# Causal mask folded into the spare rows of the maxima product, with a corner of 32 keys left, in an attention and mixture-of-experts block on one core

## The chip, the cores and the metric

The program runs on one core of a Trainium2 chip. The metric is device time in microseconds from start to end. Engines: TensorE (PE) does matrix products and transposes into PSUM, VectorE (DVE) and ScalarE (ACT) work on rows, GpSimd (POOL) does set-up work and indexed transfers, SyncE (SP) issues the other transfers.

## What is computed

One transformer block over 4 sequences of 256 tokens, width 256, 16 heads of 16, followed by 64 experts of which each token uses 8. Cut to what matters here:

```python
scores = jnp.einsum('bhqd,bhkd->bhqk', Q, K) / scale
causal = jnp.tril(jnp.ones((S, S), dtype=bool))
scores = jnp.where(causal, scores, jnp.float32(-jnp.inf))
attn = jax.nn.softmax(scores, axis=-1)
out = jnp.einsum('bhqk,bhkd->bhqd', attn, V)
...
h = _layernorm(x, axis=-1) * (1 + cb) + sb
x = x + gb * _L0_ffn_ref(h, ...)   # router, top 8 of 64 experts, silu(g) * u, down
```

## The kernel before, in words

Each engine has its own program, and semaphores order them. A prologue converts constants, normalises the first batch and projects its queries, keys and values. Batches 0 to 2 then run in rounds: a round finishes the attention of one batch and prepares the next (`one_round`, twice in a loop, then `last_round`). The attention of the last batch (3) is done tile by tile (`last_scores`, `last_values`). When all token rows are scattered by expert, the experts run, and their outputs are summed.

**Maxima.** Scores are first computed with queries on partitions (`scores_for_max`, under the mask `maskb`), and DVE takes the maximum of each row and head. `split_maxima` writes the negated maxima as a high and a low bfloat16 part to `neg2`, 2 x 16 columns of 128; the other 96 columns were set to zero once in the prologue. `neg_transposes` turns them on PE, so that row 16 c + h of the result belongs to part c of head h. ACT copies the result to `negT` in `negs` (in the last batch `last_negs`, a tile at a time).

**Scores for the values.** `attend` computes the scores once more with keys on partitions. For each of four groups of four heads it fills three PSUM banks: two with two heads each for key tile 0 (256 queries a head), one with four heads for key tile 1 (128 queries a head). In each bank PE first adds the mask to the diagonal tiles of all heads in one product (`identb` with `maskTb` broadcast over the heads), then for each head the product of keys and queries and the product of `pickb` with `negT`, which subtracts the maximum: `pickb[:, h, :]` has ones in rows h and 16 + h, in every column, and zeros elsewhere. In `attend` the mask product covers 256 columns in the banks of two heads (128 each) and 512 in the banks of four. ACT takes the exponential of each bank (`softmax`; line 684), and the banks rotate over three. `pv` on PE multiplies with the values. Between the groups ACT also does two steps for the next batch (`high`, lines 673 and 674) and copies results out (line 691).

In the last batch `last_scores` does the same for banks of four heads and one tile, with a mask product of 512 columns in the eight banks on the diagonal (line 1131), and ACT takes the exponential in `last_exp` (line 782).

**Prologue.** GpSimd converts the constants from `cst`: identity, the two masks, a prefix matrix, and `pickb` (2048 elements a row, one instruction, line 537); then it signals `g_csts`, which PE waits for before the first `neg_transposes`. In the same stretch DVE runs `rope_tile` (lines 1402, 1405, 1407) and `low` (1413, 1414) for the two tiles of batch 0. Line 1402 and 1405 read one input from PSUM and one from SBUF; 1407, 1413 and 1414 read both inputs from SBUF. PE then does the transposes of `split_transposes` (line 965), the modulation columns (line 926) and the first scores (981, 984), in that order. `link` makes an engine wait for the instruction that it is given before the next one starts.

## Time and profile before

| what | value |
|---|---|
| time, median of three runs (lowest to highest) | 316.97 us (316.59 to 317.23) |
| profiled execution, its own time | 318.18 us |
| span of that execution | 316.4 us |
| busy share PE / PE weight loads / DVE / ACT / POOL | 89% / 66% / 65% / 50% / 50% |
| mean granted clock of PE | 0.94 of 2.4 GHz |
| shares of the chain that ended last | PE 59%, DVE 15%, issue 9%, DMA 7%, ACT 4% |

A timeline lists instructions in order of time: start, duration, engine, line, operation, output and input, shape, count; in brackets the idle time of the engine before it and what ended it. Several like instructions in a row stand as one row with a count, and its duration runs from the first start to the last end. The duration of a product on PE includes its way through the array, so how long one holds PE is read from the start of the next. The granted clock is given as a share of 2.4 GHz, so 0.50 is 1.2 GHz.

### The profile page before, as it was taken

What the parts mean: (1) busy time and instruction counts of PE and PEld (TensorE: products, weight loads), DVE (VectorE), ACT (ScalarE), POOL (GpSimd) and SP (SyncE); (2) the same over time, 40 slices, a digit from 0 to 9 for tenths busy, and PEclk for the clock granted to TensorE, in tenths of its full rate; (3) what the DMA queues carried; (4) which work ended last, traced back from release to release, by engine and by line L of the source; (5) the groups of instructions that cost most, each with busy time, mean ns of one, the idle gap of its engine ahead of it and who ended that gap; (6) DMA issues with size and microseconds to landing.
All of it is one profiled execution on the core that took longest, in us unless ns stands there. A gap on an engine that the chain in (4) does not pass through costs nothing.

```text
span 316.4 us, 7008 instructions
## 1 busy us (share of the span) xinstructions
PE 282.7 (89%) x2094; PEld 208.7 (66%) x2094; DVE 205.1 (65%) x627; ACT 158.4 (50%) x462; POOL 157.7 (50%) x154
## 2 busy tenths in 40 slices
PE   6989999998999899768772759999999999999994
PEld 3478567566766667527431348888888888777883
DVE  3494876878788958852261125677777778994186
ACT  4454378545863585433621225666666666693000
POOL 1810000002555445646476564778887778888300
PEclk9795999999999999975997697999999999999999
DMA  6790099999999997992196356899998999866883
GB/s 216 260 312 1 14 309 333 338 382 294 265 265 305 312 253 223 312 322 107 58 293 204 90 137 177 169 211 192 158 163 154 181 168 153 106 75 74 178 273 133
DMA packets 63657, 64.61 MB, mean 204 GB/s; under 512 B 5069, under 2 KB 60562, under 8 KB 63632
## 3 DMA queue, kind: packets, MB, share of 16 engines
q1 hardware_dynamic: 52928, 49.07, 54.8%
q0 software_dynamic: 10704, 15.24, 25.9%
q8 instruction: 12, 0.20, 0.3%
q14 instruction: 13, 0.11, 0.1%
HBM read 35.93 MB, written 28.84 MB: 205 GB/s over the span
## 4 chain that ended last, share of the span: by engine, by line
PE 59%; DVE 15%; issue 9%; DMA 7%; ACT 4%; another core or an unknown queue 3%; POOL 1%; SPq 1%; ACTq 0%; DVEq 0%; POOLq 0%
PE bank L1280 11%; PE bank L1294 8%; PE bank L953 5%; PE bank L1271 4%; PE bank L1013 3%; PE bank L984 2%; PE bank L965 2%; PE bank L1059 2%; PE bank L1288 2%; PE bank L1029 2%; PE bank L1027 2%; PE bank L981 2%; PE bank L1024 2%; DMA arena<-in_wmod 2%
## 5 line engine op out<-in xcount | busy, mean ns | idle before, releaser
L603 POOL DMA_INDIRECT slot_rows<-stage x48 | 48.0, 999 | 37.1 <-issue 8.3
L1280 PE MATMUL bank<-arena,stage 128*128 (+1 forms) x256 | 54.1, 334 | 1.3 <-issue 1.3
L637 POOL DMA_INDIRECT sum<-kz,stage x26 | 40.1, 1542 | 10.5 <-issue 5.8
L1280 PEld LDWEIGHTS bank<-arena,stage 128*128 128x128 f32 x256 | 41.0, 194 | 2.5 <-issue 1.8
L1294 PE MATMUL bank<-arena,stage 96*128 (+1 forms) x128 | 41.0, 403 | 0.4 <-issue 0.4
L854 ACT ACTIVATE stage<-bank 128x256 f32<-128x256 f32 x64 | 24.5, 382 | 23.7 <-issue 14.6
L1430 DVE TENSOR_REDUCE rmax<-bank 128x2 f32<-128x512 f32 (+1 forms) x48 | 30.9, 686 | 7.7 <-PE bank L984 7.3
L1651 DVE SCALAR_TENSOR_TENSOR stage<-stage,bank 128x96 f32<-128x96 f32 x64 | 16.2, 253 | 24.5 <-ACT stage L864 14.1
L592 POOL COPY stage<-slot_idx 128x16 uint32<-128x16 uint32 x2 | 0.4, 196 | 59.0 <-DVE slot_idx L1529 59.0
L637 POOL DMA_INDIRECT sum<-stage x17 | 26.3, 1545 | 6.0 <-issue 3.4
L1271 PE MATMUL bank<-cst,stage 128*128 128x128 f32 x128 | 25.3, 278 | 1.3 <-DMA stage<-slot_rows 0.8
L953 PE MATMUL bank<-arena 128*128 128x512 f32 (+1 forms) x64 | 25.1, 516 | 0.5 <-ACT arena L667 0.4
L861 ACT ACTIVATE stage<-bank 128x96 f32<-128x96 f32 x64 | 16.0, 250 | 19.0 <-PE bank L1280 10.3
L1271 PEld LDWEIGHTS bank<-cst,stage 128*128 128x128 f32 x128 | 17.5, 143 | 9.9 <-issue 2.5
L1325 PE MATMUL bank<-arena 128*128 128x256 bf16 x216 | 23.7, 272 | 0.0
L1325 PEld LDWEIGHTS bank<-arena 128*128 128x128 bf16 x216 | 20.9, 97 | 2.8
L1294 PEld LDWEIGHTS bank<-arena,stage 96*128 96x128 f32 x128 | 19.4, 191 | 4.3 <-issue 0.6
L684 ACT ACTIVATE arena<-bank 128x512 f32<-128x512 f32 x36 | 20.0, 598 | 3.2 <-PE bank L1029 2.7
L981 PE MATMUL bank<-stage 128*128 128x256 bf16 (+1 forms) x48 | 16.4, 342 | 3.8 <-DVE rmax L1430 3.8
L984 PE MATMUL bank<-kz,arena 128*128 128x128 f16 (+1 forms) x128 | 19.8, 267 | 0.0
L612 POOL DMA_INDIRECT slot_rows<-rows,slot_idx x16 | 15.6, 972 | 8.5 <-issue 4.6
L1288 PE MATMUL bank<-cst,stage 128*96 128x128 f32 x64 | 18.0, 281 | 1.7 <-issue 1.0
(209 smaller groups left out, 607.6 us busy)
## 6 DMA issues: line engine op xcount, KB each, us to landing
slot_rows<-zero_row SPq DMA_DIRECT2D x8, 1040.0 KB, 12.1
stage<-slot_rows SPq DMA_DIRECT2D x64, 130.0 KB
arena<-in_gate_up SPq DMA_DIRECT2D x10, 768.0 KB
arena<-in_down SPq DMA_DIRECT2D x5, 768.0 KB
sum<-zero_row SPq DMA_DIRECT2D x3, 1152.0 KB, 13.0
arena<-sum SPq DMA_DIRECT2D x12, 256.0 KB, 4.8
arena<-in_gate_up SPq DMA_DIRECT2D x2, 864.0 KB
arena<-in_wmod SPq DMA_DIRECT2D x1, 1024.0 KB, 6.1
```

Source lines behind the costliest of these rows:

```text
L603: pool.indirect_dma_start(slot_rows, bass.IndirectOffsetOnAxis(ap=idx[:, t, k:k + 1], axis=0), src[:, t, :], None, bounds_check=last_slot, ...
L637: pool.indirect_dma_start(sums[a], where, ye_ring[e % RING], None, compute_op=ALU.add).then_inc(added[a], 16)
L854: nc.scalar.activation(xeT[:, j % 2, :], bank[j % 2][:, 0:HC * CAP], ACT.Copy).then_inc(a_xeT, 1)
L953: mm(dst, h1T[:, k, t * P:(t + 1) * P], wqkv_sb[:, k, c0:c1], start=k == 0, stop=False)
L981: mm(view[:, :, w - P:w], identb, maskb[:, None, :].broadcast_to([P, len(heads), P]), start=True, stop=False, skip_group_check=True)
L984: last = mm(view[:, i, :], qT[:, h // 2, qt * P:(qt + 1) * P], kz[:, h, 0:w], start=False, stop=i == len(heads) - 1, skip_group_check=True)
L1271: last = nc.tensor.transpose(dst, xe[:, j, k * P:(k + 1) * P], ident)
L1280: last = mm(bank[2 + q % 2][:, 0:GU + 1], xeT[:, q % 2, k * CAP:(k + 1) * CAP], expert_w[:, s - 1, k * (GU + 1):(k + 1) * (GU + 1)], start ...
L1288: nc.tensor.transpose(bank[4 + q % 2][0:I, 0:CAP], hid[:, q % 2, :], ident).then_inc(p_hidT, 1)
L1294: mm(bank[6 + q % 2][:, 0:H], hidT[:, q % 2, :], expert_w[0:I, s - 3, HC * (GU + 1):EW], start=True, stop=True).then_inc(p_ye, 1)
L1325: last = mm(dst, picked[:, n, of:of + P], y[:, n, :], start=n == 0 and y is own_high, stop=b < B - 1 and n == NPICK - 1 and y is own_low)
L1430: V.tensor_reduce(rmax[:, qt, h0:h0 + 2 * nh - 1:2], src, AX.X, ALU.max).then_inc(v_max, 1)
```

## The change

`pickb` gets ones of the identity in rows 32 to 127, for every head: row k is 1 in column k. `negT` becomes three slots of 128 columns: slot 0 for queries of tile 0, slot 1 for queries of tile 1 against keys of tile 0, slot 2 for queries of tile 1 against keys of tile 1. Rows 0 to 31 hold the maxima as before; rows 32 to 127 hold the transposed mask in slots 0 and 2 and zeros in slot 1. So the product that subtracts the maximum also masks the keys 32 to 127. Keys 0 to 31 hold a masked query only among the first 32 queries of a diagonal tile; for these a product `corner` adds the mask, 32 columns a head, behind the first head's product of keys and queries, which now opens the bank.

`neg2` has 32 columns, its zeroing on DVE is gone, the transposes write 32 rows, and ACT copies 32 rows: slots 0 and 1 in one instruction, slot 2 in another (in the last batch slot 0, and later 1 and 2). PE waits for the second copy before the first bank that reads slot 2. GpSimd fills the mask rows of `negT` and converts `pickb` in three pieces.

```diff
+    NEG = 2 * NH
...
-        neg2 = early([TPB, P // NH, NH], BF16)
-        negT = early([S], BF16)
+        neg2 = early([TPB, 2, NH], BF16)
+        negT = early([TPB + 1, P], BF16)
...
-            nc.gpsimd.tensor_copy(pickb[:, :, :], cst[:, 4 * P:4 * P + NH, None].broadcast_to([P, NH, P])).then_inc(g_csts, 1)
+            nc.gpsimd.tensor_copy(negT[:, 0, :], cst[:, 2 * P:3 * P])
+            link(nc.gpsimd.tensor_copy(negT[:, TPB, :], cst[:, 2 * P:3 * P]))
+            link(nc.gpsimd.tensor_copy(pickb[0:NEG, :, :], cst[0:NEG, 4 * P:4 * P + NH, None].broadcast_to([NEG, NH, P])))
+            link(nc.gpsimd.tensor_copy(pickb[NEG:2 * NEG, :, :], cst[NEG:2 * NEG, None, 0:P].broadcast_to([NEG, NH, P])))
+            link(nc.gpsimd.tensor_copy(pickb[2 * NEG:P, :, :], cst[2 * NEG:P, None, 0:P].broadcast_to([P - 2 * NEG, NH, P])))
+            nc.gpsimd.memset(negT[:, 1, :], 0.0).then_inc(g_csts, 1)
...
-                nc.scalar.activation(negT, bankb[0][:, 0:S], ACT.Copy).then_inc(a_negT, 1)
+                neg = bankb[0][0:NEG, 0:S].rearrange("p (t q) -> p t q", t=TPB)
+                nc.scalar.activation(negT[0:NEG, 0:TPB, :], neg, ACT.Copy).then_inc(a_negT, 1)
+                nc.scalar.activation(negT[0:NEG, TPB, :], neg[:, 1, :], ACT.Copy).then_inc(a_negT, 1)
...
+            def corner(view, n):
+
+                mm(view[:, :, 0:NEG], identb, maskTb[:, None, 0:NEG].broadcast_to([P, n, NEG]),
+                   start=False, stop=False, skip_group_check=True)
+
             def attend(b):
 
-                pe.wait_ge(a_negT, b + 1)
+                pe.wait_ge(a_negT, TPB * b + 1)
...
-                        mm(view[:, :, 0:P], identb, maskTb[:, None, :].broadcast_to([P, len(heads), P]),
-                           start=True, stop=False, skip_group_check=True)
+                        if (g, kt) == (0, 1):
+                            pe.wait_ge(a_negT, TPB * b + 2)
+                        neg = negT[:, 0:TPB, :].rearrange("p t q -> p (t q)") if kt == 0 else negT[:, TPB, :]
                         for i, h in enumerate(heads):
                             mm(view[:, i, :], kz[:, h, kt * P:(kt + 1) * P], qT[:, h // 2, kt * P:S],
-                               start=False, stop=False, skip_group_check=True)
-                            last = mm(view[:, i, :], pickb[:, h, :], negT[:, kt * P:S],
+                               start=i == 0, stop=False, skip_group_check=True)
+                            if i == 0:
+                                corner(view, len(heads))
+                            last = mm(view[:, i, :], pickb[:, h, :], neg,
...
-                if t == kt:
-                    mm(view, identb, maskTb[:, None, :].broadcast_to([P, 4, P]),
-                       start=True, stop=False, skip_group_check=True)
...
+                    if t == kt and i == 0:
+                        corner(view, 4)
...
-            pe.wait_ge(a_negT, B + 1)
+            pe.wait_ge(a_negT, TPB * (B - 1) + 3)
...
-            link(V.memset(neg2[:, :, :, :], 0.0))
```

GpSimd in the prologue, before; `stage` and `arena` are the buffers that hold the converted constants:

```order
L532 MEMSET arena 128x32 [waits v_zeroed]
L533 CAST stage<-cst 128x128
L534 CAST stage<-cst 128x128
L535 CAST stage<-cst 128x128
L536 CAST stage<-cst 128x128
L537 CAST stage<-cst 128x2048
L542 COPY arena<-router_sb 128x32 [waits wo_and_router_loaded]
```

and after:

```order
L537 CAST stage<-cst 128x128
L538 CAST stage<-cst 128x128
L539 CAST stage<-cst 128x128
L540 CAST stage<-cst 32x2048 [waits gpsimd_chain]
L541 CAST stage<-cst 32x2048 [waits gpsimd_chain]
L542 CAST stage<-cst 64x2048 [waits gpsimd_chain]
L543 MEMSET stage 128x128 [waits gpsimd_chain]
L548 COPY arena<-router_sb 128x32 [waits wo_and_router_loaded]
```

In the place of one conversion of 2048 elements a row stand two of 128 elements, three of 2048 and a memset, and the long ones wait for one another (`gpsimd_chain`).

PE in the first bank of `attend` and the start of the second, before; `stage` holds `identb`, `pickb`, `negT`, the mask, `arena` the queries, `kz` the keys:

```order
L1024 MATMUL bank<-stage 128x2x128 [waits neg_max_T_ready]
L1027 MATMUL bank<-arena,kz 128x256
L1029 MATMUL bank<-stage 128x256
L1027 MATMUL bank<-arena,kz 128x256
L1029 MATMUL bank<-stage 128x256
L1024 MATMUL bank<-stage 128x2x128
```

and after:

```order
L1042 MATMUL bank<-arena,kz 128x256 [waits neg_max_T_ready]
L1008 MATMUL bank<-stage 128x2x32
L1046 MATMUL bank<-stage 128x256
L1042 MATMUL bank<-arena,kz 128x256
L1046 MATMUL bank<-stage 128x256
L1042 MATMUL bank<-arena,kz 128x256
L1008 MATMUL bank<-stage 128x2x32
```

The mask product of 256 columns at the head of the bank has become one of 64 columns in second place; the number of products in a bank is the same.

## Rows read from the trace of the kernel before

**Rows 1.** Timeline of PE in the second attend: start us, us, engine, line, operation.
```profile
73.98 0.28 PE L1024 MATMUL bank<-stage 128*128 128x256 bf16 x1 [0.48 <-ACT stage L744]
74.10 0.27 PE L1027 MATMUL bank<-arena,kz 128*128 128x256 f16 x1
...
75.08 0.38 PE L1024 MATMUL bank<-stage 128*128 128x512 bf16 x1
75.30 0.22 PE L1027 MATMUL bank<-arena,kz 128*128 128x128 f16 x1
75.35 0.22 PE L1029 MATMUL bank<-stage 128*128 128x128 bf16 x1
```

**Rows 2.** Timeline of ACT in the second attend.
```profile
73.54 0.38 ACT L744 ACTIVATE stage<-bank 128x256 bf16<-128x256 bf16 x1 [2.58 <-PE bank L993]
74.74 3.56 ACT L684 ACTIVATE arena<-bank 128x512 f32<-128x512 f32 x6 [0.81 <-PE bank L1029]
...
79.24 1.71 ACT L684 ACTIVATE arena<-bank 128x512 f32<-128x512 f32 x3
...
82.36 1.57 ACT L684 ACTIVATE arena<-bank 128x512 f32<-128x512 f32 x3
```

**Rows 3.** All instructions of line 684: count, then shortest/median/longest in ns.
```profile
L684 ACT ACTIVATE arena<-bank x36: 585/597/618, 42.5 to 116.1; 128x512 f32<-128x512 f32 x36
```

**Rows 4.** Timeline of PE just before the second attend, products of 64 columns.
```profile
71.16 0.19 PE L1093 MATMUL bank<-stage,onesb 128*128 128x64 bf16 x1
71.19 0.19 PE L1092 MATMUL bank<-stage 128*128 128x64 bf16 x1
```

**Rows 5.** Timeline of PE in the last batch.
```profile
145.25 0.63 PE L1131 MATMUL bank<-stage 128*128 128x512 bf16 x1
145.68 0.31 PE L1134 MATMUL bank<-arena,kz 128*128 128x128 f16 x1
```

**Rows 6.** The chain that ended last, in the last batch: start us, us, what.
```profile
153.40 0.59 ACT arena L782
```

**Rows 7.** Timeline of POOL in the prologue.
```profile
6.88 0.28 POOL L507 CAST arena<-arena 8x128 bf16<-8x128 f32 x1 [5.88 <-DMA arena<-in_bias]
...
14.43 0.29 POOL L536 CAST stage<-cst 128x128 bf16<-128x128 f32 x1
14.66 1.89 POOL L537 CAST stage<-cst 128x2048 bf16<-128x2048 f32 x1
```

**Rows 8.** Timeline of DVE in the prologue.
```profile
14.66 0.88 DVE L1405 TENSOR_TENSOR arena<-bank,rope_sb 128x256 f32<-128x256 f32 x2
15.58 1.52 DVE L1407 TENSOR_TENSOR arena<-arena 128x512 f32<-128x512 f32 x1
...
19.50 0.69 DVE L1413 TENSOR_TENSOR arena<-arena 128x512 f16<-128x512 f32 x1
...
21.55 0.69 DVE L1414 TENSOR_TENSOR arena<-arena 128x512 f16<-128x512 f32 x1
...
34.11 0.17 DVE L1570 TENSOR_SCALAR rs<-mv 128x4 f32<-128x4 f32 x1 [0.62 <-ACT arena L753]
```

**Rows 9.** All instructions of line 1407, shortest/median/longest in ns.
```profile
L1407 DVE TENSOR_TENSOR arena<-arena x8: 692/693/1516, 15.6 to 111.4; 128x512 f32<-128x512 f32 x8
```

**Rows 10.** Timeline of PE in the prologue.
```profile
22.30 1.54 PE L965 MATMUL bank<-stage,arena 128*128 128x128 f16 x16 [0.18 <-DVE arena L1414]
23.63 3.52 PE L926 MATMUL bank<-condT,arena 128*128 128x4 f32 x16
```

**Rows 11.** Timeline of ACT in the prologue.
```profile
30.63 1.02 ACT L667 ACTIVATE arena<-bank,modT 128x256 f32<-128x256 f32 x2 [4.33 <-PE bank L943]
```

**Rows 12.** PE by stretch: us, PE busy (instructions), granted clock, DMA share, GB/s.
```profile
22.50:23.00 0.50, 0.50 (x11) 0.72 0.81 243
...
32.50:33.00 0.50, 0.50 (x3) 0.54 0.00 0
...
149.00:149.50 0.50, 0.50 (x11) 0.98 0.17 58
```

More of the change, by code:

```diff
@@ L792, in last_negs @@
                 act.wait_ge(p_negT, B + t)
-                q = slice(t * P, (t + 1) * P)
-                nc.scalar.activation(negT[:, q], bankb[(3, 0)[t]][:, q], ACT.Copy).then_inc(a_negT, 1)
+                neg = bankb[(3, 0)[t]][0:NEG, t * P:(t + 1) * P]
+                for slot in ((0,), (1, TPB))[t]:
+                    nc.scalar.activation(negT[0:NEG, slot, :], neg, ACT.Copy).then_inc(a_negT, 1)
             def one_round(it, more):
@@ L992, in neg_transposes @@
                 for t in range(TPB):
-                    last = nc.tensor.transpose(bankb[0][:, t * P:(t + 1) * P],
+                    last = nc.tensor.transpose(bankb[0][0:NEG, t * P:(t + 1) * P],
                                                neg2[:, t, :, :].rearrange("p c h -> p (c h)"), identb)
                 last.then_inc(p_negT, 1)
+            def corner(view, n):
+                mm(view[:, :, 0:NEG], identb, maskTb[:, None, 0:NEG].broadcast_to([P, n, NEG]),
+                   start=False, stop=False, skip_group_check=True)
             def attend(b):
-                pe.wait_ge(a_negT, b + 1)
+                pe.wait_ge(a_negT, TPB * b + 1)
                 n = 0
@@ L1129, in last_scores @@
                 view = bank[1 + n % 2 if n < 4 else 4 + n % 3][:, :].rearrange("p (h q) -> p h q", q=P)
-                if t == kt:
-                    mm(view, identb, maskTb[:, None, :].broadcast_to([P, 4, P]),
-                       start=True, stop=False, skip_group_check=True)
                 for i, h in enumerate(groups[g]):
                     mm(view[:, i, :], kz[:, h, kt * P:(kt + 1) * P], qT[:, h // 2, t * P:(t + 1) * P],
-                       start=t != kt and i == 0, stop=False, skip_group_check=True)
-                    last = mm(view[:, i, :], pickb[:, h, :], negT[:, t * P:(t + 1) * P],
+                       start=i == 0, stop=False, skip_group_check=True)
+                    if t == kt and i == 0:
+                        corner(view, 4)
+                    last = mm(view[:, i, :], pickb[:, h, :], negT[:, t + kt, :],
                               start=False, stop=i == 3, skip_group_check=True)
@@ L1159, in last_neg_transposes @@
                     pe.wait_ge(a_rows, B - 1)
-                nc.tensor.transpose(bankb[(3, 0)[t]][:, t * P:(t + 1) * P],
+                nc.tensor.transpose(bankb[(3, 0)[t]][0:NEG, t * P:(t + 1) * P],
                                     neg2[:, t, :, :].rearrange("p c h -> p (c h)"), identb).then_inc(p_negT, 1)
@@ L1180, in last_round @@
                 scores_for_max(it, 8, 9, b)
-                pe.wait_ge(a_negT, B)
+                pe.wait_ge(a_negT, TPB * (B - 1) + 1)
                 last_scores(0)
```

## The prediction

> **What bounds the kernel now.** I read the chain that ended last first, then the timelines of TensorE (PE), ScalarE (ACT), VectorE (DVE) and GpSimd (POOL) in the three places that the change touches, and last the granted clock. The attention part (about 10 to 165 us) is one chain of dependent steps that passes from engine to engine; the expert part starts when the last rows are scattered. So a microsecond gained or lost on that chain should reach the end, and one gained beside it should not.
>
> In one call of attend PE begins at 73.98, right behind ACT's copy of the negated maxima [rows 1, 2]. A product of 256 columns holds PE 0.11 us, one of 128 columns 0.055, and the mask product of 512 columns 0.22 (75.08 to 75.30) [rows 1]. One group of four heads, which is three banks, takes PE two times 5 x 0.11 plus 0.22 plus 8 x 0.055, so 1.75 us. ACT takes the exponentials of the same banks, 0.59 each [rows 3], with some overlap. The last three of the call took 1.57 in all [rows 2], so they came every (1.57 - 0.59) / 2 = 0.49: ACT's own pace. The first six took 3.56, one every (3.56 - 0.59) / 5 = 0.59, which is PE's pace, 1.75 / 3. The middle three took 1.71, one every 0.56. So attend is bound by PE in its first half and by ACT in its second, and the two are close.
>
> In the prologue the chain runs over DVE. It rotates and splits queries and keys (14.66 to 22.24) [rows 8]; PE then transposes them, does the modulation columns and the first scores without a gap (from 22.30 on) [rows 10].
>
> **The change in attend.** Every bank loses a mask product over all its columns and gets a corner of 32 columns a head. A bank of two heads goes from 256 to 64 columns, one of four heads from 512 to 128. A product of 64 columns, with a weight load of its own, is followed by the next one 0.03 us later [rows 4], one of 128 columns 0.055 later [rows 1]. The number of weight loads is unchanged. So PE saves 0.08 on each of eight banks and 0.16 on each of four, 1.28 us for one attend. A group then costs PE 1.43, which is just under ACT's 3 x 0.49 = 1.47: ACT is late next, and what comes out is what ACT lost to PE. That is 0.08 at the first bank, 6 x (0.575 - 0.49) = 0.51 over the first six (3.45 from first start to the end at ACT's pace, 3.56 less one overlap of 0.1), and about 0.13 over the middle three. Together 0.72, **2.2 us less** for three calls. The bounds are 3 x 0.08 = 0.25 (ACT's spacing is its own) and 3 x 1.28 = 3.8 (all of PE's saving counts); I stay with the value between, since the last three show ACT's pace with its banks ready.
>
> The price there is a second copy on ACT, for the third slot of negT. The copy of 256 columns takes 0.38 and ends at 73.92; the first exponential starts at 74.74 [rows 2]. The new one has half the columns, costs 0 to 0.38 and lies inside these 0.82 us. Only the third bank waits for it, and PE is there about 0.9 us after the first copy. Queued behind it on ACT is the first exponential, which waits for PE anyway. I count nothing; in the last batch, where PE waits for both copies before the fifth bank, it may cost up to 0.38 and has PE's transposes beside it. The transposes that now write 32 rows stream as many columns as before: nothing. The removed memset on DVE is worth 0 to 0.17 (the shortest DVE operation in [rows 8]); I count nothing.
>
> **The change in the last batch.** Eight mask products of 512 columns become corners of 128. The one at 145.25 stands in a stretch at half clock and holds PE 0.43 [rows 5]; a quarter of that is 0.11, so it saves 0.32. Two more stand ahead of the exponential at 153.40, for which the chain waits [rows 6], at 0.22 - 0.055 = 0.16 each. Together **0.65 us less**. The other five stand beside waits for other engines; in full they would give 5 x 0.16 = 0.8 more, which I keep as a bound.
>
> **The change in the prologue.** GpSimd used to convert pickb in one instruction of 1.89 us [rows 7]. Now it is three, for 32, 32 and 64 rows, each with the same 2048 elements a row, each waiting for the one before. The time goes by elements in a row and not by rows: 8 rows of 128 took 0.28, 128 rows of 128 took 0.29 [rows 7]. So I take 1.89 for each. Ahead of them come two more conversions of 128 columns, 0.24 apart. GpSimd thus works from 14.66 to about 21.5 and not to 16.55.
>
> That costs because of one row of DVE. The addition in line 1407 has both inputs in SBUF; it takes 0.69 normally [rows 9], and took 1.52 at 15.58, while GpSimd's conversion ran until 16.55 [rows 7, 8]. It ended at 17.10, 0.55 after that conversion: it was held until GpSimd was through. The operations of line 1405, which read one input from PSUM, ran at 14.66 beside the same conversion at 0.44 each [rows 8], and were not held.
>
> Worked out for the new order: the first conversion runs from 15.26 to 17.15, and the addition, ready at 15.58, ends at 17.7 and not 17.1. The second conversion waits for it and runs to about 19.45. The next addition, ready at 19.36, gets through by 20.05; the third conversion starts then and ends at 21.85. The subtractions of lines 1413 and 1414, both inputs in SBUF, were to start at 20.1: the first is held and ends at 22.4. The last ends at 24.4, where it ended at 22.24: 2.2 us. If GpSimd never waits for DVE, the second addition is held instead, and the same 2.2 comes out. The bounds are 0 and 2.8 (held at every one of the three conversions).
>
> The Trainium skill, SBUF — State Buffer, section Who interferes with whom, has a rule that speaks against this change: a VectorE instruction with two SBUF inputs and a GpSimd instruction that reads SBUF exclude each other, and whichever starts first keeps the port for its whole length. The trace agrees with 1.52 against 0.69 in one direction; no row here shows the other. By the rule the delay is the 2.2 above; were the port shared by halves, each held operation would lose half its overlap, and it would be about 1.
>
> Then PE. Its clock falls to 1.2 GHz at 22.7, after PE had waited for DVE, and is back at 2.4 GHz at 32.95 [rows 12]. Both groups of 16 transposes now lie wholly in the slow stretch, at 0.107 each (0.43 / 4, [rows 5]), so the modulation columns start at 23.1 + 3.4 = 26.5 and not 23.63 [rows 10], 2.9 late. If the clock comes back at 32.95 as before, the first scores and the transposes behind them catch up a little: ACT's step at 30.63 [rows 11] begins about 33.15, DVE's step at 34.11 [rows 8] as much later, and attend begins **2.4 us later**. If the clock comes back later by as much as the work is late, it is 3.1.
>
> **The clock in the last batch.** There PE is at 1.2 GHz until 149.0 [rows 12]. The work is 2.4 - 2.2 = 0.2 late there; a rise that stays at 149.0, as I took the one at 32.95 to stay, leaves 0.2 us less of dense work at half speed, **0.1 less**.
>
> **The sum.** +2.4 - 2.2 - 0.65 - 0.1 = -0.55, some -0.5. The profiled execution took 318.18 with a span of 316.4, so it would be 317.7; against the median of the three runs, 316.97, it is **316.5 us**, no change, or just faster. A measurement of this kernel can tell about 0.2%, 0.63 us, from no change.
>
> **The rivals.** (1) In attend the saving lies beside ACT: its spacing of 0.59 is its own, and only the first bank counts. +2.4 - 0.25 - 0.65 = +1.5, so 318.5, slower. For it: ACT is hardly ever idle there; against it: 0.49 in the last three. It decides from the point where the first six exponentials still take over 3.4. (2) The clock's rise follows the work in the prologue: +3.1 - 2.2 - 0.65 = +0.25, 317.2, the same. For it: both rises came in dense work; against it: nothing in the rows ties them to the program. (3) GpSimd's conversions hold DVE hardly at all, and the one long addition was chance. Then -2.2 - 0.65 = -2.85, of which a rise at 149.0 that stays takes back up to half of 2.2: 314.1 to 315.2, faster. Against it is that the addition ended just behind GpSimd. (4) The five other masks of the last batch count too: -0.55 - 0.8 = -1.35, 315.6, faster. Against it: PE pauses in those stretches. That the change does not bring what it says is rival 1.
>
> **Chances.** The forecast 0.34 (its own range is 315.9 to 317.1); rival 1 0.18; rival 2 0.17; rival 3 0.14; rival 4 0.17. Faster: 0.13 of the forecast, 0.14 of rival 3, 0.15 of rival 4, that is 0.42. Slower: 0.16 of rival 1, 0.06 of rival 2, that is 0.22. The rest, 0.36, is the same. The range, 315.0 to 318.3, takes in rivals 2 and 4 whole, the near ends of rivals 1 and 3, and the bounds next to them.
>
> **What would show it.** In the trace after: three long conversions on GpSimd and, beside them, additions and subtractions of DVE that take over 1 us; the last subtraction ending near 24.4; the first attend starting 2.4 later; the first six exponentials in about 3.0; some 9.2 us from attend's first product to its last exponential's end and not 9.95 (73.98 to 83.93). The forecast is wrong if DVE ends near 22.3, if attend keeps its length, or if the clock's edges move with the work.

## The result and the profile after

The first comparison gave 324.22 us as the median of four executions of the changed kernel (322.40 to 325.78), against 317.1 for the kernel before (four executions, 316.59 to 321.58); the ratio is 1.0203, with an interval of 1.0142 to 1.0263. The profiled execution of the changed kernel took 322.4 us with a span of 320.5, where the one of before had 318.18 and 316.4. Four later comparisons, with both kernels timed in turn on one chip each, give much less: ratios of 0.9974, 0.9968, 1.0072 and 1.0041, on average 1.0014, and differences of means from -0.04% to +0.9%, with a weighted mean of **+1.2 us and a standard error of 0.4**. (The ratios leave out executions more than 1.5% above a kernel's fastest; the differences of means take in all but one stray one.) The four sets differ by more than their own errors (-0.1 ± 0.7 and +3.0 ± 0.8 us at the ends), so the 0.4 is too narrow. The change thus brings no gain: it makes the kernel slower by 0.1 to 0.4%, which isn't clear of nothing by the ratios, and the larger part of the first figure belongs to that set of executions.

The page of after, first its head, then TensorE's and GpSimd's busy time (share of the span, instructions):

```profile
span 320.5 us, 7016 instructions
...
PE 279.2 (87%) x2094; PEld 207.4 (65%) x2094; DVE 205.6 (64%) x626; ACT 157.6 (49%) x466; POOL 163.0 (51%) x159
```

TensorE is busy 3.5 us less than before and GpSimd 5.3 more: both halves of the change are there. Where the two stand in the prologue, GpSimd first, then DVE (start us, us, engine, line, operation), after:

```profile
15.53 1.89 POOL L540 CAST stage<-cst 32x2048 bf16<-32x2048 f32 x1
17.48 2.23 POOL L541 CAST stage<-cst 32x2048 bf16<-32x2048 f32 x1
19.77 2.31 POOL L542 CAST stage<-cst 64x2048 bf16<-64x2048 f32 x1
...
15.77 2.19 DVE L1423 TENSOR_TENSOR arena<-arena 128x512 f32<-128x512 f32 x1
...
19.64 0.69 DVE L1423 TENSOR_TENSOR arena<-arena 128x512 f32<-128x512 f32 x1
20.36 2.27 DVE L1429 TENSOR_TENSOR arena<-arena 128x512 f16<-128x512 f32 x1
...
24.02 0.69 DVE L1430 TENSOR_TENSOR arena<-arena 128x512 f16<-128x512 f32 x1
```

These answer to [rows 7, 8]. The additions and subtractions of 0.69 take 2.19 and 2.27 where a conversion is running, and the conversions of 1.89 take 2.23 and 2.31 where DVE is ahead. The last subtraction ends at 24.71 (before: 22.24). TensorE behind it, after:

```profile
18.69 1.95 PE L935 MATMUL bank<-condT,arena 128*128 128x4 f32 x16
23.53 3.57 PE L974 MATMUL bank<-stage,arena 128*128 128x128 f16 x32 [2.89 <-DVE arena L1430]
26.90 3.52 PE L935 MATMUL bank<-condT,arena 128*128 128x4 f32 x16
30.28 0.59 PE L990 MATMUL bank<-stage 128*128 128x512 bf16 x1
```

It now waits 2.89 us for DVE, all 32 transposes run at half clock, and the modulation columns begin at 26.90, where they began at 23.63 [rows 10]. The granted clock is the last number but two, after:

```profile
32.50:33.00 0.50, 0.50 (x6) 0.50 (x5) 0.38 (x1) 0.00 (x0) 0.00 (x0) 0.50 0.00 0
36.00:36.50 0.50, 0.50 (x2) 0.17 (x2) 0.43 (x3) 0.47 (x2) 0.00 (x0) 0.76 0.00 0
```

So TensorE is back at 2.4 GHz at 36.2, not at 32.95 as before [rows 12]. ScalarE in the second attend, after:

```profile
76.20 0.37 ACT L751 ACTIVATE stage<-bank 32x256 bf16<-32x256 bf16 x1 [2.58 <-PE bank L1002]
76.48 0.25 ACT L752 ACTIVATE stage<-bank 32x128 bf16<-32x128 bf16 x1
77.30 3.04 ACT L690 ACTIVATE arena<-bank 128x512 f32<-128x512 f32 x6 [0.57 <-PE bank L1046]
...
81.32 1.55 ACT L690 ACTIVATE arena<-bank 128x512 f32<-128x512 f32 x3
...
84.24 0.60 ACT L697 ACTIVATE arena<-bank 128x512 f32<-128x512 f32 x1 [0.33 <-PE bank L1027]
84.74 1.57 ACT L690 ACTIVATE arena<-bank 128x512 f32<-128x512 f32 x3
```

Against [rows 2] the six exponentials take 3.04 and not 3.56, the next three 1.55 and not 1.71; but ahead of the last three there is now a pause of 0.33.

How the lateness of the profiled execution develops (after less before): +2.47 at the last subtraction, +3.26 at the first copy of negated maxima on ACT, +2.46 at the third, +1.81 at ACT's first step behind the third attend, +2.35 at the last exponential of the last batch, +2.64 where the last slots (the places of the token rows among the experts) are ready, +2.95 at ACT's first copy for the experts, +4.1 at the end. ACT at these points, the first copy, the third, the step behind the third attend and the last exponential, before:

```profile
40.69 0.38 ACT L744 ACTIVATE stage<-bank 128x256 bf16<-128x256 bf16 x1 [4.24 <-PE bank L993]
...
106.00 0.38 ACT L744 ACTIVATE stage<-bank 128x256 bf16<-128x256 bf16 x1 [2.58 <-PE bank L993]
...
126.72 0.20 ACT L656 ACTIVATE rs<-rs 128x2 f32<-128x2 f32 x1 [3.06 <-DVE rs L1479]
...
155.63 0.58 ACT L782 ACTIVATE arena<-bank 128x512 f32<-128x512 f32 x1
```

and after:

```profile
43.95 0.37 ACT L751 ACTIVATE stage<-bank 32x256 bf16<-32x256 bf16 x1 [4.24 <-PE bank L1002]
...
108.46 0.37 ACT L751 ACTIVATE stage<-bank 32x256 bf16<-32x256 bf16 x1 [2.63 <-PE bank L1002]
...
128.53 0.20 ACT L662 ACTIVATE rs<-rs 128x2 f32<-128x2 f32 x1 [3.05 <-DVE rs L1495]
...
157.98 0.58 ACT L790 ACTIVATE arena<-bank 128x512 f32<-128x512 f32 x1
```

The prologue costs over 3 us, the three calls of attend bring 1.45 back (0.60, 0.20, 0.65), and the last batch loses 0.54. The last 1.75 us arise behind the attention, where no instruction was changed; what makes them is not shown.

### The profile page after: what moved, and what is told of

It is laid out like the page before. It is cut to its first block, busy times and chain, and to the rows that moved or that the text cites. A ratio compares the mean times of both kernels' runs of the same rounds, so it can differ in the third digit from the quotient of the medians.

```text
span 320.5 us, 7016 instructions
## 1 busy us (share of the span) xinstructions
PE 279.2 (87%) x2094; PEld 207.4 (65%) x2094; DVE 205.6 (64%) x626; ACT 157.6 (49%) x466; POOL 163.0 (51%) x159
## 4 chain that ended last, share of the span: by engine, by line
PE 56%; DVE 13%; issue 12%; DMA 7%; ACT 6%; another core or an unknown queue 2%; POOL 1%; SPq 1%; ACTq 0%; DVEq 0%; POOLq 0%
PE bank L1296 11%; PE bank L1310 7%; PE bank L962 5%; PE bank L1287 4%; PE bank L993 3%; PE bank L1027 3%; PE bank L974 3%; ACT arena L690 2%; PE bank L990 2%; PE bank L1304 2%; PE bank L1076 2%; DMA arena<-sum 2%; PE bank L1100 2%; DMA arena<-in_wmod 2%
## 5 line engine op out<-in xcount | busy, mean ns | idle before, releaser
L870 ACT ACTIVATE stage<-bank 128x96 f32<-128x96 f32 x64 | 16.1, 251 | 19.3 <-PE bank L1296 12.3
L1287 PEld LDWEIGHTS bank<-cst,stage 128*128 128x128 f32 x128 | 17.5, 143 | 10.2 <-issue 2.3
L915 PE MATMUL bank<-onesb 128*128 128x512 bf16 x49 | 17.0, 515 | 4.0 <-DVE slot_idx L1545 2.9
L690 ACT ACTIVATE arena<-bank 128x512 f32<-128x512 f32 x36 | 18.7, 614 | 2.1 <-PE bank L1046 2.1
```

Source lines behind the costliest of these rows:

```text
L690: nc.scalar.activation(dst, bank[4 + n % 3][:, :], ACT.Exp, scale=SCALE).then_inc(a_exp, 1)
L1287: last = nc.tensor.transpose(dst, xe[:, j, k * P:(k + 1) * P], ident)
```

## The experiments

Each set ran on a chip of its own, beside the kernel before. "Mean" is the mean of all executions less that of the kernel before, with its standard error.

| set | kernel | executions | median us | before, median | ratio (interval) | mean us |
|---|---|---|---|---|---|---|
| 1 | e1_late | 12 | 318.06 | 319.20 | 0.9916 (0.9867 to 0.9965) | -1.3 ± 0.7 |
| 1 | e2_convert | 12 | 323.16 | 319.20 | 1.0108 (1.0059 to 1.0157) | +3.0 ± 0.6 |
| 1 | e3_before_late | 12 | 319.20 | 319.20 | 1.0015 (0.9969 to 1.0062) | +0.4 ± 0.7 |
| 1 | e4_after_again | 12 | 318.38 | 319.20 | 0.9974 (0.9934 to 1.0015) | -0.1 ± 0.7 |
| 2 | f1_after_third | 10 | 322.99 | 321.06 | 0.9968 (0.9911 to 1.0025) | +1.6 ± 1.0 |
| 2 | f2_before_itself | 10 | 320.47 | 321.06 | 0.9995 (0.9958 to 1.0032) | -0.4 ± 0.5 |
| 2 | f3_late_pause | 4 | 318.53 | 321.06 | 0.9863 (0.9777 to 0.9949) | -3.0 ± 1.2 |
| 2 | f4_after_warm | 10 | 320.63 | 321.06 | 0.9967 (0.9922 to 1.0013) | -0.6 ± 0.7 |
| 3 | g1_late_held | 6 | 318.20 | 321.66 | 0.9888 (0.9820 to 0.9956) | -3.2 ± 0.8 |
| 3 | g2_after_held | 12 | 322.74 | 321.66 | 0.9968 (0.9922 to 1.0014) | +1.2 ± 0.9 |
| 3 | g3_before_held | 12 | 320.38 | 321.66 | 0.9946 (0.9897 to 0.9995) | -0.6 ± 0.8 |
| 4 | h1_after_fifth | 12 | 321.12 | 318.14 | 1.0072 (1.0022 to 1.0123) | +3.0 ± 0.8 |
| 5 | i1_after_warm5 | 12 | 318.67 | 319.32 | 1.0025 (0.9977 to 1.0074) | -0.3 ± 0.8 |
| 5 | i2_after_beside | 12 | 320.02 | 319.32 | 1.0041 (0.9986 to 1.0097) | +1.3 ± 0.9 |
| 5 | i3_late_again | 12 | 316.34 | 319.32 | 0.9952 (0.9905 to 0.9998) | -1.9 ± 0.8 |

### Prologue and masks apart

e1_late is the changed kernel with GpSimd's conversions behind DVE's work on the first batch:

```diff
+            pool.wait_ge(v_xn, 2)
             nc.gpsimd.tensor_copy(negT[:, 0, :], cst[:, 2 * P:3 * P])
```

> The changed kernel, with GpSimd's two mask conversions, the three conversions of pickb and the memset held back until DVE has normalised batch 1 (about 24 us before the change), where DVE reads PSUM. Theory A, the held DVE operations in the prologue and the clock that returns later behind them cost the time: the last subtraction (line 1430) ends near 22.3 and not 24.7, the first attend starts near 41 and not 45.1, and the masks' saving of about 2 us comes out: 314 to 316 us, under the kernel before. Theory B, the loss arises in the last batch or in the expert part from the other instruction order: 320 us or more, with the first attend near 41 all the same.

e2_convert is the kernel before with GpSimd's conversions of the changed one alone (the masks stay as they were; the extra copies go into unused tiles):

```diff
-            nc.gpsimd.tensor_copy(pickb[:, :, :], ...).then_inc(g_csts, 1)
+            nc.gpsimd.tensor_copy(spare0, cst[:, 2 * P:3 * P])
+            link(nc.gpsimd.tensor_copy(spare1, cst[:, 2 * P:3 * P]))
+            link(nc.gpsimd.tensor_copy(pickb[0:32, :, :], ...))
+            link(nc.gpsimd.tensor_copy(pickb[32:64, :, :], ...))
+            link(nc.gpsimd.tensor_copy(pickb[64:P, :, :], ...))
+            nc.gpsimd.memset(spare0, 0.0).then_inc(g_csts, 1)
```

> The kernel before, with only GpSimd's prologue of the changed one: two conversions of 128 columns into a spare buffer, pickb in three linked pieces with the same content as before, and a memset. Theory A: the first attend starts 3.4 us later as in the changed kernel, 320 to 321 us or more. Theory B: the delay is absorbed on the way, 317 us.

e3_before_late is the kernel before with the wait of e1_late ahead of its own conversion; e4_after_again is the changed kernel unchanged.

> The kernel before, with its one conversion of pickb held back until DVE has normalised batch 1. Theory A: the addition of line 1407 takes 0.69 and not 1.52, DVE is 0.8 us earlier, 316.1 us, and if the clock's edges stay at their times up to as much again is lost or gained. Theory B: no change, 317 us. Against the first run it shows what the masks alone bring: A expects about 2.5 us between the two.

> The changed kernel once more, beside the others on one chip. Its four runs lay between 322.4 and 325.8. A: the same, with the spread from slow spells of the clock that come or stay away in the last batch and at the start of the experts; a chip that behaves otherwise would give a tighter spread.

Measured: the prologue alone costs +3.0 us (e2_convert), the masks alone bring -1.3 (e1_late), moving before's own conversion nothing that can be measured (e3_before_late), both together -0.1. Against e3_before_late, the comparison that was to show the masks alone, e1_late gains 1.7 ± 0.9, where theory A had about 2.5; with the masks in place the early conversions cost 1.2 ± 0.9 (e4_after_again less e1_late). The two halves add up to 1.7 and not to -0.1, a gap of 1.8 with an error of 1.1. The 322.4 to 325.8 of the first comparison did not come again here: e4_after_again ran from 315.89 to 322.20. In e2_convert's trace GpSimd and DVE stand as in after:

```profile
17.29 2.40 POOL L541 CAST stage<-cst 32x2048 bf16<-32x2048 f32 x1
...
20.33 2.26 DVE L1419 TENSOR_TENSOR arena<-arena 128x512 f16<-128x512 f32 x1
```

Its last subtraction ends at 24.68 and its first copy of negated maxima comes at 43.92 (after: 24.71 and 43.95), and not a mask is changed in it. So the first half of the forecast's mechanism stands. e1_late, with its last subtraction at 22.95 and its first copy at 38.60, fell short of the 314 to 316 that theory A expected for it.

### How far the first figure can be had again

f1_after_third and h1_after_fifth are the changed kernel, f2_before_itself the kernel before.

> The changed kernel itself, a third time, beside the kernel before. Theory A (the prologue costs about 3.4 us, the mask products give about as much back; the first comparison's 1.0203 came of two sets of runs at different levels) expects a ratio between 0.995 and 1.005 here, so -1.5 to +1.5 us. Theory B (the change costs 6 to 7 us on most chips, and the second comparison was the exception) expects 1.015 to 1.025.

> The kernel before, compared with itself: what this comparison shows where there is no difference. Theory A expects a ratio of 1.000 within 0.004, and a spread of single runs of about 8 us (315 to 323) for both. If the ratio is off by 0.5% or more, differences of that size between two sets of runs mean nothing, and theory B's 1.02 is the less telling.

> The changed kernel once more beside the kernel before. In its 26 runs so far its time goes with the mean granted clock of the execution (-1.8 us for each 0.01 more, correlation -0.84): 324 to 326 at 0.918 to 0.93, 316 to 319 at 0.945 to 0.96; the kernel before has the same slope at half the size. Theory A (the change is worth about nothing, and the first comparison's 4 runs, at a mean clock of 0.928, fell in the slow kind by chance) expects both kinds again, those under 0.932 at 322 or more and those over 0.945 under 321, and a mean within 2 us of the kernel before's. Theory B (the change costs 6 us) expects nearly all runs over 322 and a mean 5 us or more above.

f2_before_itself gives 0.9995, so the comparison itself is sound. The changed kernel gives -0.1, +1.6, +3.0 and, with i2_after_beside, +1.3 us: theory B's 5 to 7 us falls. Theory A's "nothing" fits three of the four within twice their errors, and not h1_after_fifth; there, too, two of the six executions with a clock under 0.932 were under 322, against theory A. The level varies as well: 128 executions of the kernel before in the five sets run from 314.86 to 325.43 with a median of 319.7, and only 23 of them are at or under the 317.23 that was the slowest of the three which the prediction started from. Of the 50 executions of the changed kernel, 15 took 322.4 or more, as all four of the first set did; so that set lay at the high end of the one kernel, and three of the four of before at the low end of the other. In those 50 the time falls by 1.8 us for each 0.01 of mean granted clock (correlation -0.83), and h1_after_fifth had 0.932 where the kernel before had 0.950. The price thus goes from set to set with the clock that the executions got (e4_after_again, with -0.1 us, had 0.947 where the kernel before had 0.948).

### Hold or clock

f4_after_warm and i1_after_warm5 give TensorE something to do in the pause ahead of the transposes, i2_after_beside and i3_late_again are after and e1_late on the same chip:

```diff
             mod_columns(4, 8)
+            keep_warm(13)
             pe.wait_ge(g_csts, 1)
```

(5 in place of 13 for i1_after_warm5).

> The changed kernel with 13 products of 512 columns of ones (2.8 us at full clock) on TensorE while it waits for the split queries and keys, at 20.6 to 23.5; their result is not used. GpSimd's and VectorE's part stays as in after: the last subtraction ends at 24.7. Theory A (2.3 of the 3.4 us come of VectorE being held, the rest of the clock coming back later) expects that the clock doesn't fall at 22.6, that the first copy of negated maxima on ScalarE comes 15.65 us behind the last subtraction as in e1_late, at 40.4 and not 43.95, and a time 2 to 4 us under f1_after_third. If the spell at half clock comes nonetheless, or if the time until attend stays at 19.2 us behind the subtraction, the clock is not what costs there.

> The changed kernel with 5 products of 512 columns of ones on TensorE (1.1 us at full clock, 1.8 at half) in its pause of 1.4 to 2.9 us ahead of the transposes; so they end before the transposes can begin, unlike the 13 of f4_after_warm. Their result is not used. VectorE stays held: last subtraction at 24.7. Theory C (the spell at half clock is most of the price) expects no spell or one of 3.4 us from 22 to 25 on, 15.6 to 16.1 us from the last subtraction to the first copy of negated maxima instead of 18.8 to 19.2, so this copy at 40.3 to 40.8 and not 43.4 to 44.3, and a time 2 to 3.5 us under i2_after_beside. Theory V (the held VectorE is the price, the clock is by the way) expects a time within 1 us of i2_after_beside. If the spell comes nonetheless, the trace decides nothing on its price.

> The changed kernel on the same chip, for comparison with the other two. Theory C and theory V both expect +0 to +3 us against the kernel before, ratio 1.000 to 1.010, as in the three sets of ten and twelve runs so far; 18.8 to 19.3 us from the last subtraction to the first copy of negated maxima.

> e1_late again on this chip: GpSimd's conversions late, neither hold nor long spell. Both theories expect 3 to 4.5 us under i2_after_beside, ratio to the kernel before 0.988 to 0.997; theory C expects it 0.5 to 2.5 us under i1_after_warm5 (the hold alone), theory V 3 us or more under it.

f4_after_warm failed as an experiment. Its products came late, the clock fell at 23.75 just behind the first of them, and 13 took 4.65 us, so the transposes waited for them:

```profile
23.63 4.65 PE L915 MATMUL bank<-onesb 128*128 128x512 bf16 x13
28.12 1.95 PE L974 MATMUL bank<-stage,arena 128*128 128x128 f16 x32
```

Its first copy of negated maxima came at 44.17, 19.07 behind the last subtraction. Its time is 2.2 ± 1.1 us under f1_after_third's, as theory A expected, but the trace does not show it gained by the way that theory A names; so the run speaks for neither.

i1_after_warm5 did what was meant. DVE is held as in after (last subtraction at 24.64), TensorE's five products end before the transposes start, and the granted clock stays at 1.00. TensorE, then the stretch from 26 to 27, then ACT's first copy of negated maxima:

```profile
21.78 1.24 PE L915 MATMUL bank<-onesb 128*128 128x512 bf16 x5
23.46 1.05 PE L974 MATMUL bank<-stage,arena 128*128 128x128 f16 x16 [0.44 <-DVE arena L1431]
```

```profile
26.00:27.00 1.00, 1.00 (x11) 1.00 (x11) 0.96 (x3) 0.97 (x2) 0.00 (x0) 1.00 0.00 0
```

```profile
39.53 0.37 ACT L751 ACTIVATE stage<-bank 32x256 bf16<-32x256 bf16 x1 [4.24 <-PE bank L1002]
```

The same stretch in h1_after_fifth, where TensorE has nothing to do ahead of its transposes (it is of another set: i2_after_beside, the changed kernel on i1_after_warm5's chip, had only 3.4 us at half clock in its profiled execution and the copy 15.71 behind the subtraction, where 18.8 to 19.3 was expected):

```profile
23.58 1.05 PE L974 MATMUL bank<-stage,arena 128*128 128x128 f16 x16 [1.39 <-DVE arena L1430]
```

```profile
26.00:27.00 1.00, 1.00 (x10) 1.00 (x7) 0.96 (x3) 0.98 (x2) 0.00 (x0) 0.50 0.00 0
```

Both begin their transposes within 0.12 us of each other; the first negated maxima come at 39.53 and at 43.39. Over the profiled executions, all but f4_after_warm's, the time from the last subtraction to that copy goes with how long TensorE was at half clock in this stretch (f4_after_warm had 3.4 us and 19.07, since its transposes stood behind the added products):

| at half clock | executions | us from subtraction to copy |
|---|---|---|
| not at all | e1_late, f3_late_pause, i3_late_again, g3_before_held, i1_after_warm5 | 14.9 to 15.7 |
| 3.4 us | f2_before_itself, e3_before_late, g1_late_held, i2_after_beside | 15.7 to 16.1 |
| 10.2 us | before, f1_after_third, g2_after_held, h1_after_fifth | 18.45 to 18.8 |
| 13.7 us | after, e2_convert, e4_after_again | 19.2 |

So the long spells cost some 3 to 4 us there. With GpSimd's early conversions and no extra products (after, e2_convert, e4, f1, g2, h1, i2) one was there in six executions of seven; with the conversion of before, or late ones (before, f2, e3, g3, e1, f3, g1, i3), in one of eight, and that one is the execution that the prediction was read from. In times, on one chip: i2_after_beside less i1_after_warm5 is 1.6 ± 1.0 us, which would be the clock's part; i1_after_warm5 less i3_late_again is 1.6 ± 0.9, the part of the held DVE. The first lies between what theory C (2 to 3.5) and theory V (under 1) expected of the clock. Neither part is clear of its error by itself, only their sum of 3.2 ± 1.1 is; that it falls into halves is an estimate, and of i1_after_warm5's twelve executions only the profiled one shows that the spell stayed away.

### A stall that looked like the sink of the gain

e1_late has its last slots ready 8.7 us earlier than after, and yet its first expert comes no earlier. ScalarE, behind its table load, in f1_after_third, which has the same stall, and then in after:

```profile
173.89 1.28 ACT L854 ACT_TABLE_LOAD   x1
191.42 0.66 ACT L863 ACTIVATE stage<-bank 128x256 f32<-128x256 f32 x2 [16.24 <-remote]
```

```profile
176.80 1.28 ACT L854 ACT_TABLE_LOAD   x1
184.62 0.38 ACT L863 ACTIVATE stage<-bank 128x256 f32<-128x256 f32 x1 [6.54 <-PE bank L1287]
```

In e1_late, e3_before_late and f1_after_third ACT does nothing for 16.1 to 16.2 us, 8 to 9 us past the transposes that it copies; in those three alone GpSimd issues its last 18 scatters without a pause of even a microsecond. Four kernels were meant to make GpSimd pause there:

```diff
                 scatter_last(1, k, g_last[k])
+                if k == 2:
+                    pool.wait_ge(a_xeT, 1)
```

(as shown in g1_late_held, g2_after_held and g3_before_held, on top of e1_late, of the changed kernel and of the kernel before; f3_late_pause is e1_late with such a wait behind k == 0, for p_xeT, TensorE's first transposes.)

> The changed kernel with GpSimd's conversions late (as in e1_late), and GpSimd pausing behind the first of the last ten scatters until TensorE has transposed the first expert's rows. In e1_late the last slots were ready at 169.25 (after: 177.91), but ScalarE's first copy of the expert part came only at 185.77, 8.7 us after its transposes, while GpSimd issued scatters without a gap from 157.30 to 182.91. Theory P (ScalarE's start into the expert part is held while GpSimd issues scatters back to back) expects that copy right behind the transposes, at about 176, the first expert 8 to 9 us earlier than in e1_late and about 5 us earlier than after, and a time of 310 to 314. Theory Q (ScalarE is held by something else that doesn't depend on the scatters) expects the copy at 184 to 186 as before, and a time like e1_late's, 317 to 319.

> The changed kernel with GpSimd's conversions late (as in e1_late), and GpSimd holding its last seven scatters until ScalarE has made its first copy of the expert part. In e1_late, e3_before_late and f1_after_third ScalarE did nothing for 16.1 to 16.2 us behind its table load (169.67 to 185.79 in e1_late) though its input was ready 8 to 9 us earlier, and GpSimd issued scatters all that time; in the other runs GpSimd had a pause of about 4 us there and ScalarE went on as soon as its input was ready. Theory P (ScalarE is held as long as GpSimd issues scatters without a pause) expects that the idle time behind the table load is 6 to 8 us in every run, the first expert's copy within 0.2 us of its transposes, and a time of 312 to 315.5, ratio 0.975 to 0.990. Theory Q (something else holds ScalarE for 16 us) expects that GpSimd now waits for ScalarE too: the last scatter goes out at about 195 and not 183, and the time is 318 to 323.

> The changed kernel with the same hold of the last seven scatters, and nothing else. Theory P (the runs of 323.7 to 326 of the changed kernel, the first comparison's among them, are those in which GpSimd has no pause and ScalarE is held) expects that none of the runs is over 322 and the median falls by 0 to 3 us against f1_after_third's, to 317 to 319.5 beside a kernel before of 319 to 321. Theory Q expects runs up to 326 as before, and a median 0 to 3 us higher.

> The kernel before with the same hold alone, which tells what the hold itself costs or gives where the change isn't made. Theory P expects -2 to 0 us against the kernel before (it takes away the same idle time in those runs of before that have it), ratio 0.994 to 1.000; theory Q 0 to +3 us, since scatters of the last seven experts of the first eight go out later.

None of the four profiled executions shows the long stall, but in all four GpSimd had its pause of about 4 us ahead of the added wait anyway, as in after. So they don't tell theory P from theory Q. The times of theory P did not come either, 318.5 and 318.2 in f3_late_pause and g1_late_held for the 310 to 314 and 312 to 315.5 expected, though g1_late_held's ratio and g3_before_held's are in its ranges. What falls is P's second claim: g2_after_held still had executions up to 327.3, so the stall is not what makes the changed kernel's longest executions. In f3_late_pause the wait took something for itself, 4.93 us in which the second expert waited for its rows. What makes ACT stop is open.

## Why the prediction was wrong, point by point

**GpSimd holds DVE (+2.2 at the last subtraction).** Right in the mechanism and nearly in size: 2.47, with the conversions at 1.89 where no DVE operation is ahead of them. The two operations that were to be held, the first addition and the first subtraction, are the two that were. Over all profiled executions the last subtraction ends at 24.60 to 25.10 in the nine with the early conversions and at 21.25 to 23.14 in the eight others. The 1.52 of the kernel before, from which the prediction read the hold, is of one execution: in f2_before_itself and g3_before_held, with the same conversion, the addition begins behind it and takes 0.69. The Trainium skill's rule that was weighed there (SBUF — State Buffer, Who interferes with whom: whoever starts first keeps the shared port for the whole instruction) is borne out in both directions, 2.27 against 0.69 on DVE and 2.31 against 1.89 on GpSimd. Sharing by halves is out: 2.27 is longer than twice 0.69.

**Attend starts 2.4 later, with the clock back at 32.95.** This step failed. The clock came back at 36.2, and the first copy of negated maxima was 3.3 late. Of the 0.9 too much, 0.3 is the hold's (2.47 for 2.2), so the rest, by this estimate, is the clock's. Rival 2 had 3.1 for it and a chance of 0.17. The cause lies one step further back: the rise doesn't stand at a time of its own, and neither does the fall. They differ between executions of one kernel (f2_before_itself has 3.4 us at half clock where before had 10.2), and with the early conversions a long spell was there in six executions of seven. The length of TensorE's wait ahead of its transposes doesn't decide it alone: i2_after_beside waited 2.93 us and had 3.4 at half clock, before waited 0.61 and had 10.2. What decides in one execution stays open. The prediction took the spell of one execution for a fixed part of both kernels. In times the prologue costs +3.0 ± 0.6 without the masks (e2_convert); with them the early conversions cost 1.2 ± 0.9, 3.2 ± 1.1 and 4.5 ± 1.1 against late ones (e4_after_again less e1_late, i2_after_beside less i3_late_again, g2_after_held less g1_late_held). The forecast was 2.4; these figures have 3 in their middle, with a wide spread.

**Attend (-0.72 a call, -2.2).** The pace was right: the six exponentials in 3.04 (3.0 was forecast), PE and ACT about level. From the first product to the last exponential's end the first call took 9.19 and not 9.95 us, as forecast; the second took 9.68, since ACT pauses 0.33 ahead of L697, as it does in the third. The product that is named there had long been done, so what ends the pause isn't known. From one copy of negated maxima to the next the two rounds gained 0.60 and 0.20, and to ACT's first step behind it the third attend gained 0.65: 1.45 in place of 2.2.

**The last batch (-0.65).** The products shrank as forecast: the one at half clock holds PE 0.10, those at full clock 0.055. But this step failed too. The stretch from the third copy of negated maxima to the last exponential, third attend included, took 49.52 us where it had taken 49.63, so some 1.4 us of forecast saving left 0.1; behind the third attend 0.54 was lost where 0.65 was to be gained. At the first exponentials PE was not what ACT waited for. The last product ahead of the first exponential of the last batch, and that exponential, before:

```profile
132.54 0.22 PE L1136 MATMUL bank<-stage 128*128 128x128 bf16 x1
...
132.89 0.60 ACT L782 ACTIVATE arena<-bank 128x512 f32<-128x512 f32 x1 [1.91 <-PE bank L1136]
```

The same and the next exponential, after:

```profile
134.20 0.22 PE L1152 MATMUL bank<-stage 128*128 128x128 bf16 x1
...
136.26 0.60 ACT L790 ACTIVATE arena<-bank 128x512 f32<-128x512 f32 x1 [3.65 <-PE bank L1152]
139.14 0.60 ACT L790 ACTIVATE arena<-bank 128x512 f32<-128x512 f32 x1 [2.28 <-remote]
```

The product ends at 134.42, the exponential begins 1.84 us later (before: 132.76 and 132.89, 0.13 later). Such stops of ACT, which the waits in the trace do not explain, stand in both kernels in this part, at other places and of other lengths in each execution; what PE saves ahead of one is lost in it.

**The clock in the last batch (-0.1).** The rise came at 148.9, where the forecast had 149.0. That is luck: the clock had fallen at 142.1 and not at 138.8, so the spell was 6.8 us and not 10.2, and nothing was gained by it.

In times, the masks bring -1.3 ± 0.7 and -1.9 ± 0.8 beside the kernel before (e1_late, i3_late_again), -1.7 ± 0.9 beside e3_before_late, -3.1 ± 0.8 beside e2_convert (e4_after_again) and -2.6 ± 1.0 (g1_late_held less g3_before_held): about 2.2, where the forecast had 2.95.

**The sum.** +2.4 - 2.95 was -0.55; with the measured terms it is +3.0 - 2.2 = +0.8, and the direct comparisons give +1.2 ± 0.4 by the means and some +0.5 by the ratios. Each term was off by 0.6 to 0.8 to the same side, and that turned the sign of a small difference of two larger numbers. The rest of the gap to 324.22 is the level: 316.97 was the median of three executions at the low end of what the kernel before does, and the range of 315.0 to 318.3 had no room for a spread that goes from 315 to 325. The 0.2% that the prediction gave a measurement came of these three executions and is far too small.

**A version that beats both** is e1_late: 0.9916 and 0.9952 of the kernel before on two chips (e1_late, i3_late_again), under 1%, and 1.2 ± 0.9 and 3.2 ± 1.1 us under the changed kernel, together 2.0 ± 0.7: the masks without the hold. With a hold of the last scatters (g1_late_held, f3_late_pause) it was at 0.9888 and 0.9863; these intervals overlap with its own.

## What to carry to other kernels

When a change puts work on GpSimd beside DVE operations with both inputs in SBUF, price the whole overlap, and then ask what TensorE does in the pause that follows: here a long spell at the lower clock took 3 to 4 us of the prologue in the profiled executions. A setup conversion that nobody needs for 20 us belongs behind the first critical stretch. A few idle products in an unavoidable pause may pay, if they end before the real work comes; the 1.6 ± 1.0 us that they brought here isn't clear of its error. A difference of two terms of 2 to 3 us in a kernel whose executions scatter by 10 needs both kernels side by side on more than one chip, and an execution's clock spells are not to be read as the program's.

## What the chip showed that was not expected

The same prologue has different times at half clock from execution to execution: 0, 3.4 or 10.2 us with the instructions of before (g3_before_held, f2_before_itself, before), 3.4, 10.2 or 13.7 with those of the changed kernel. The time of the whole goes with the mean granted clock, 1.8 us for 0.01 in the changed kernel and 1.1 in the kernel before (correlations -0.83 and -0.51). A small DVE operation is held as long as a large one: with the conversions moved behind, one on 16 columns took 1.75 us in e1_late, where its neighbours take 0.17 to 0.23, beside a conversion that ended at 31.36. (The same section of the Trainium skill, SBUF — State Buffer, Who interferes with whom, counts tensor_scalar among the operations that can take the shared port if their operands allow it; the trace agrees, with 1.75 against 0.17 to 0.23.)

```profile
29.64 1.75 DVE L1394 TENSOR_SCALAR arena<-arena 128x16 f32<-128x16 f32 x1
31.43 0.23 DVE L1395 TENSOR_SCALAR arena<-arena 128x16 f32<-128x16 f32 x1
```

And ScalarE can stand still for 16 us behind a table load with its input ready, in three of seventeen profiled executions.
